# Attention and feed-forward sandwich: one inversion for the norm of the next input and of the output, input statistics in step 0

## The chip, the cores and the metric

The kernel runs on one core of a Trainium2 chip. The metric is the device time of one execution in microseconds (us). The core has five instruction queues that run side by side and meet in semaphores: TensorE (PE, matrix products and transposes; PEld is its weight load), VectorE (DVE), ScalarE (ACT), GpSimd (POOL) and SyncE (SP, which only issues DMA transfers).

## What is computed

Sixteen inputs of 256 tokens by 256 channels go through one attention layer and one feed-forward layer. Each layer is wrapped in two layer norms: one on what goes in, one on what comes out, before it is added to the residual.

```
x = x + _layernorm(attn(_layernorm(x)))
x = x + _layernorm(ffn(_layernorm(x)))

attn: q = x @ Wq.T (16 heads of 128); kv = x @ Wkv.T; kv_head = cumsum(x @ Wkvh.T * exp(cumsum of log_sigmoid(x @ Wg.T)))
      k, v = one key and one value row per token, scaled for each head by kv_head
      q, k = rope(q), rope(k); p = softmax(q k^T / sqrt(128), causal); out = (p v) @ Wout.T
_layernorm: (x - mean) / sqrt(var + 1e-5)
```

All 16 inputs are of one kind, so the attention part is a loop over 16 batches.

## The kernel before

Attention runs in 128 units, each a pair of heads: 16 batches of 8 pairs. The program is written out by hand as one stream of steps. A batch that begins at unit g0 (a multiple of 8) has steps s = 0 to 7, and every engine runs through the same steps in its own fixed order, with semaphores between. In step s a pair is projected and gets its cosine, the pair before is scored, the one before that goes through softmax, and older ones are transposed, multiplied with the values and projected out (table LAG).

Within one step the engines have this work for the pairs:

- TensorE: transposes of the probabilities (L944 to L946), value products, query projection, scores (L927, L929), output projection.
- VectorE: reciprocal of the sums (L1575), low half of the output (o_lo, L1597), query cosine (L1550), four splits of the probabilities (L1588), the maxima with the mask (L1562 to L1565).
- ScalarE: the exponents (L1229, L1231), the high halves, and the swap of the query halves (L1217, L1218).
- GpSimd: queries times sine (L597, waits for the swap), the rope addition (L607, which the scores wait for), normalise (L631, waits for L1575), keys times head scale (L620).

Around this stream lie the rarer pieces. Each has a step number in a table: FRONT for the batch that comes next, AHEAD for the batch after it (its norm is made early), TAIL for the outputs of the batch before. Of AHEAD there are the statistics of x (L1445, L1450 on VectorE; steps 3 and 4), the inversion (`invert_x`, L551 to L558 on GpSimd; step 5) and the normalisation on ScalarE (steps 6 and 7). Of TAIL there are the statistics of the attention output y (L1529, L1534; step 7), its inversion (`invert_y`, L575 to L582; step 1 of the next batch), its normalisation (steps 3 and 4) and the residual (L588; step 6). An inversion is four instructions on 2 columns, one for each block of 128 tokens: variance plus epsilon, mean times -1, the power -0.5, and the bias as the product. The mean and the inverse deviation of x and of y lie in the same tile `small`, not side by side.

A third stream makes the ternary weights of the feed-forward part, one chunk in two batches: on VectorE the steps above (L1622, even batches, step 1), below (L1630, even, start of step 2), decide (L1639, even, start of step 6), sign (L1646, odd, start of step 0), change (L1654) and finish (L1661, odd, steps 1 and 2), each on 1024 columns with two inputs in SBUF; on TensorE the transposes of the chunk in step 7 of odd batches (3 to 13). "Even" and "odd" are batch numbers, counted from 0; batch 8 begins at g0 = 64.

Of the kernel before, what the change touches and what calls it, by code (L numbers as in the profile page):

```python
# [25 lines left out]
ALU = mybir.AluOpType  # L26
AX = mybir.AxisListType

P = 128
# [25 lines left out]
             decay_a=3, decay_b=4, coef=5, weigh=5, sum=5, store=6, made=5, taken=5, turned=6, values_hi=7, values_lo=7, vh=7)  # L55
AHEAD = dict(stats_a=3, stats_b=4, invert=5, norm_a=6, norm_b=7)
FIRST = dict(stats_a=0, stats_b=0, invert=0, norm_a=1, norm_b=1, turn=2, split=2, split_lo=3, keys=3, gates=4,
# [26 lines left out]
def sandwich_kernel(nc, x, wq, wkv, wkvh, wg, wout, wgu, wproj, rope, out):  # L84
    ctx = ExitStack()
    with ctx:
# [20 lines left out]
        ones = sb("ones", [P, 1])  # L107
        minus_half = sb("minus_half", [P, NT])
        eps = sb("eps", [P, 1])
# [101 lines left out]
        ln1_stat = small[:, 48:60].rearrange("p (t a) -> p t a", a=6)  # L211
        ln1_agg = small[:, 60:64].rearrange("p (t a) -> p t a", a=2)
        ln1_rstd = small[:, 64:66]
        ln2_stat = small[:, 66:78].rearrange("p (t a) -> p t a", a=6)
        ln2_agg = small[:, 78:82].rearrange("p (t a) -> p t a", a=2)
        ln2_rstd = small[:, 82:84]
        gate_mark = small[:, 84:86]
        ln1_minus, ln2_minus = small[:, 90:92], small[:, 92:94]
        ln1_bias, ln2_bias = small[:, 86:88], small[:, 88:90]

# [91 lines left out]
        def front_at(g0, s, stage):  # L312

            if g0 == 0 and FIRST.get(stage) == s:
                return PAIRS
            if g0 + 2 * PAIRS < STEPS and AHEAD.get(stage) == s:
                return g0 + 2 * PAIRS
            if 0 < g0 and g0 + PAIRS < STEPS and FRONT.get(stage) == s:
                return g0 + PAIRS

        def tail_at(g0, s, stage):

            if g0 == STEPS and TAIL_LAST[stage] == s:
                return g0 - PAIRS
            back = TAIL[stage] // PAIRS
            if TAIL[stage] % PAIRS == s and g0 >= (back + 1) * PAIRS and (g0 < STEPS or back):
                return g0 - (back + 1) * PAIRS

        def head_count(g, j):
# [202 lines left out]
        def _(pool):  # L532
# [14 lines left out]
            def invert_x(c0):  # L547
# [10 lines left out]
                nc.gpsimd.tensor_tensor(ln1_bias, ln1_minus, ln1_rstd, ALU.mult).then_inc(ln1_biased, PAIRS)  # L558

            def key_sin(c0):  # L560

# [10 lines left out]
            def invert_y(c0):  # L572
# [4 lines left out]
                nc.gpsimd.tensor_tensor(ln2_minus, ln2_agg[:, :, 0], minus_one, ALU.mult).then_inc(ln2_neg, PAIRS)  # L577
                pool.wait_ge(ln2_eps, c0 + PAIRS)
                nc.gpsimd.tensor_tensor(ln2_rstd, ln2_rstd, minus_half[:, 0:NT], ALU.pow).then_inc(ln2_inv, PAIRS)  # L579
                pool.wait_ge(ln2_inv, c0 + PAIRS)  # L580
                pool.wait_ge(ln2_neg, c0 + PAIRS)
                nc.gpsimd.tensor_tensor(ln2_bias, ln2_minus, ln2_rstd, ALU.mult).then_inc(ln2_biased, PAIRS)  # L582
# [138 lines left out]
            def batch(g0, par, steps):  # L721
                for s in range(steps):
# [10 lines left out]
                    if not is_first(g0, s) and not is_first(g0, s - 2) and not is_first(g0, s - 3):  # L733
                        normalise(g0, s)
                        scale_keys(g0, par, s)
                    c0 = front_at(g0, s, "invert")
                    if c0 is not None:
                        invert_x(c0)
                    c0 = tail_at(g0, s, "invert")
                    if c0 is not None:  # L740
                        invert_y(c0)
# [404 lines left out]
        def _(act):  # L1146
# [16 lines left out]
            def norm_y(c0, tiles):  # L1163

                act.wait_ge(ln2_biased, c0 + PAIRS)
                act.wait_ge(x1_done, c0 + PAIRS)
# [748 lines left out]
```

## Time and profile before

| what | us |
|---|---|
| median of three runs (lowest, highest) | 1044.86 (1044.78, 1045.16) |
| the profiled execution, its own time | 1044.8 |
| its span, first to last instruction | 1043.0 |
| TensorE busy in the span | 1025.7 |
| GpSimd busy in the span | 937.8 |
| ScalarE and VectorE busy in the span | 868.6 and 824.8 |

TensorE's granted clock is 0.998 of full over the span. The attention batches run to about 823 us, the feed-forward part takes the rest. In a table of the profile "busy" is the time in which an instruction of the engine was under way; TensorE's products overlap each other, so that it can be busy throughout and still have waited a little before one of them. The timeline gives each instruction's start in us from the span's start.

### The profile page before, as it was taken

To read this page: it belongs to the slowest core of one execution; us is meant where nothing else is said; L and a number is where in the kernel's file an instruction comes from. 1 tells how busy PE (TensorE), PEld (TensorE's weight loads), DVE (VectorE), ACT (ScalarE), POOL (GpSimd) and SP (SyncE) were. 2 spreads that over 40 slices of the span, in tenths; PEclk is the share of its full clock that TensorE was granted. 3 is DMA by queue.
4 is the path that set the end of the run, shared out by engine and by line. 5 is a ranking of instruction groups with operands and counts; after the bars stand their busy time and mean duration, and the time that the engine had idled before them with its cause. 6 is when DMAs were issued, how large, how long until landed. Compare 5 with 4: busy or idle time off the path is not lost.

```text
span 1043.0 us, 25125 instructions
## 1 busy us (share of the span) xinstructions
PE 1025.7 (98%) x7859; PEld 985.8 (95%) x7859; DVE 824.8 (79%) x2824; ACT 868.6 (83%) x2399; POOL 937.8 (90%) x927
## 2 busy tenths in 40 slices
PE   7999999999999999999999999999999999999996
PEld 6899999999999999999999999999999899999996
DVE  6868798878887888888788888887777756766665
ACT  5978898989898889898988898888878777777774
POOL 4889999999999999999999999999999758888776
PEclk9999999999999999999999999999999999999999
DMA  7551111112111111221121112111131000000001
GB/s 262 186 183 42 41 63 41 43 52 72 42 32 62 62 42 33 65 66 44 38 76 43 42 52 62 50 34 63 31 113 31 2 1 12 30 24 22 21 22 41
DMA packets 35124, 58.56 MB, mean 56 GB/s; under 512 B 3136, under 2 KB 16000, under 8 KB 34688
## 3 DMA queue, kind: packets, MB, share of 16 engines
q1 hardware_dynamic: 34992, 56.96, 17.1%
q8 instruction: 63, 1.03, 0.4%
q14 instruction: 69, 0.57, 0.2%
HBM read 50.92 MB, written 9.18 MB: 58 GB/s over the span
## 4 chain that ended last, share of the span: by engine, by line
POOL 57%; PE 21%; issue 14%; DVE 1%; ACT 1%; POOLq 0%; ACTq 0%; DVEq 0%
POOL arena L597 15%; POOL arena L620 13%; POOL arena L631 13%; POOL arena L607 12%; PE psum L1015 12%; PE psum L1053 6%; PE psum L773 2%; POOL arena L579 1%; POOL arena L555 1%; POOL X L588 1%; PE psum L1028 1%; PE psum L1037 0%; POOL arena L563 0%; DVE pt_split L1588 0%; POOL wo_lo L648 0%
## 5 line engine op out<-in xcount | busy, mean ns | idle before, releaser
L631 POOL TENSOR_TENSOR arena<-arena 128x768 f32<-128x768 f32 x128 | 196.3, 1533 | 9.6 <-DVE arena L1575 9.0
L607 POOL TENSOR_TENSOR arena<-arena 128x512 f32<-128x512 f32 x128 | 174.6, 1364 | 10.0
L1588 DVE SCALAR_TENSOR_TENSOR pt_split<-psum,vh_col,pt_split 128x256 fp32r<-128x256 f32 (+1 forms) x512 | 177.0, 407 | 2.9 <-ACT pt_split L1248 2.7
L597 POOL TENSOR_TENSOR arena<-arena,tables 128x512 f32<-128x512 f32 x128 | 165.5, 1293 | 15.2 <-ACT arena L1218 14.4
L620 POOL TENSOR_TENSOR arena<-arena 128x512 f32<-128x512 f32 x127 | 163.0, 1284 | 0.0
L927 PE MATMUL psum<-arena 128*128 128x256 f32 x512 | 154.0, 382 | 3.8 <-POOL arena L607 2.5
L1229 ACT ACTIVATE arena<-arena 128x256 f32<-128x256 f32 x256 | 128.6, 502 | 28.4 <-DVE arena L1565 22.3
L773 PE MATMUL psum<-wo_hi,o_hi 128*128 128x256 f32 x512 | 152.0, 297 | 0.0
L773 PE MATMUL psum<-xt_lo,wq_hi 128*128 128x256 f32 x512 | 144.5, 282 | 0.0
L773 PE MATMUL psum<-xt_hi,wq_lo 128*128 128x256 f32 x512 | 144.4, 282 | 0.0
L773 PE MATMUL psum<-wo_hi,o_lo 128*128 128x256 f32 x512 | 144.2, 282 | 0.0
L773 PE MATMUL psum<-xt_hi,wq_hi 128*128 128x256 f32 x512 | 144.0, 281 | 0.0
L773 PE MATMUL psum<-wo_lo,o_hi 128*128 128x256 f32 x512 | 143.6, 281 | 0.0
L773 PE MATMUL psum<-pt_split,vals_hi 128*128 128x512 f32 (+1 forms) x512 | 142.3, 359 | 0.2
L1015 PE MATMUL psum<-xt_hi,wq_hi 128*128 128x256 f32 x512 | 125.6, 282 | 0.0
L1015 PE MATMUL psum<-xt_lo,wq_hi 128*128 128x256 f32 x512 | 124.4, 284 | 0.0
L1247 ACT ACTIVATE pt_split<-psum,vh_col 128x256 fp32r<-128x256 f32 x256 | 120.7, 472 | 0.1
L1217 ACT ACTIVATE arena<-psum 64x512 f32<-64x512 f32 x128 | 76.1, 595 | 46.6 <-DVE arena L1550 45.3
L1597 DVE TENSOR_TENSOR o_lo<-psum,o_hi 128x512 fp32r<-128x512 f32 x128 | 87.4, 682 | 33.9 <-ACT o_hi L1257 32.8
L929 PEld LDWEIGHTS psum<-arena 128*128 128x128 f32 x512 | 97.2, 190 | 13.3
L1563 DVE CUSTOM_DVE_ANT_0 arena<-psum,mask 128x256 f32<-128x256 f32 x256 | 107.0, 418 | 0.0
L1231 ACT ACTIVATE arena<-arena 128x128 f32<-128x128 f32 x256 | 99.4, 388 | 0.0
(193 smaller groups left out, 3415.8 us busy)
## 6 DMA issues: line engine op xcount, KB each, us to landing
arena<-kh_rows SPq DMA_DIRECT2D x127, 256.0 KB, 3.3
out<-spare SPq DMA_DIRECT2D x15, 256.0 KB, 2.2
arena<-w_rows SPq DMA_DIRECT2D x6, 512.0 KB, 4.7
X<-L_attn_Wout SPq DMA_DIRECT2D x1, 2048.0 KB, 14.5
X<-L_attn_x SPq DMA_DIRECT2D x1, 2048.0 KB, 12.3
arena<-L_attn_Wq SPq DMA_DIRECT2D x1, 1536.0 KB, 10.3
X<-L_attn_x SPq DMA_DIRECT2D x1, 1536.0 KB, 9.5
w_rows<-L_ffn_w_gate_up SPq DMA_DIRECT2D x3, 512.0 KB, 7.7
```

What stands on the lines that cost most here:

```text
L597: nc.gpsimd.tensor_tensor(swap, swap, spread, ALU.mult).then_inc(q_sined, 1)
L607: nc.gpsimd.tensor_tensor(q_rot[p % 2], q_cos[p % 2], q_swap[p % 2], ALU.add).then_inc(q_roped, 1)
L620: nc.gpsimd.tensor_tensor(k_head[p % 2], keys[par].unsqueeze(1).to_broadcast([P, HP, N]), kh_all[p % 4], ALU.mult).then_inc(k_scaled, 1)
L631: nc.gpsimd.tensor_tensor(tb, tb, r.unsqueeze(3).to_broadcast([P, HP, 3, P]), ALU.mult).then_inc(p_ready, 1)
L773: last = nc.tensor.matmul(o, a, b, start=start and i == 0, stop=stop and i == len(passes) - 1, skip_group_check=skip)
L927: nc.tensor.matmul(sj[:, 0:2 * P], q[:, j, P:N], kt[:, j, :], start=True, stop=True, skip_group_check=True)
L1015: last = nc.tensor.matmul(bank[c % 2 * 2 + half][:, j * N:(j + 1) * N], wgu_t[:, k, col:col + P], part[:, k, :], start=n == 0 and j == 0, ...
L1229: nc.scalar.activation(tb[:, j, 0:2 * P], tb[:, j, 0:2 * P], ACT.Exp, scale=-1.0, bias=nmax[p % 4][:, 2 * j:2 * j + 1], accum_out=rsum[p % ...
L1231: nc.scalar.activation(tb[:, j, 2 * P:3 * P], tb[:, j, 2 * P:3 * P], ACT.Exp, scale=-1.0, bias=nmax[p % 4][:, 2 * j + 1:2 * j + 2], accum_ ...
L1247: nc.scalar.activation(pt_hi[p % 2][:, j * N:(j + 1) * N], b[:, 0:N], ACT.Copy, scale=vh[:, 0, h:h + 1])
L1563: nc.vector.tensor_tensor_reduce(tb[:, j, 0:2 * P], S_BANK[j][:, 0:2 * P], mask[:, :], -1.0, -MASKED, ALU.add, ALU.min, nmax[p % 4][:, 2 * ...
L1588: last = nc.vector.scalar_tensor_tensor(pt_lo[p % 2][:, o], b[:, i], vh[:, t, h:h + 1], pt_hi[p % 2][:, o].bitcast(F32), ALU.mult, ALU.sub ...
```

## The change

The statistics of the next input go from steps 3 and 4 to step 0, and its inversion from step 5 to step 1, where that of the output already is. Batch 0 keeps the old steps (AHEAD_FIRST). Where both inversions fall in one step, which is in batches 2 to 13, they are made by one group of four instructions on 4 columns (`invert_both`); the means, variances and results of x and y lie side by side for that. In batch 1 there is only x to invert, in batches 14 and 15 and after them only y; these keep groups of two columns. ScalarE's normalisation of y then waits on the semaphore of the common group. `Y_ALONE` makes up the counts.

```diff
-AHEAD = dict(stats_a=3, stats_b=4, invert=5, norm_a=6, norm_b=7)
+AHEAD = dict(stats_a=0, stats_b=0, invert=1, norm_a=6, norm_b=7)
+AHEAD_FIRST = dict(stats_a=3, stats_b=4, invert=5, norm_a=6, norm_b=7)
+Y_ALONE = STEPS - 4 * PAIRS
...
+        ln_agg = small[:, 72:80].rearrange("p (t a) -> p t a", a=2)
+        ln_rstd, ln_bias, ln_minus = small[:, 80:84], small[:, 86:90], small[:, 90:94]
+        ln1_agg, ln2_agg = ln_agg[:, 0:NT, :], ln_agg[:, NT:2 * NT, :]
...
-            if g0 + 2 * PAIRS < STEPS and AHEAD.get(stage) == s:
+            if g0 + 2 * PAIRS < STEPS and (AHEAD if g0 else AHEAD_FIRST).get(stage) == s:
...
+            def invert_both(c0, y0):
+
+                pool.wait_ge(ln1_aggr, c0 + PAIRS)
+                pool.wait_ge(ln2_aggr, y0 + PAIRS)
+                at_least(pool, ln1_done, c0)
+                at_least(pool, ln2_done, y0 + PAIRS)
+                nc.gpsimd.tensor_tensor(ln_rstd, ln_agg[:, :, 1], eps[:, 0:1].to_broadcast([P, 2 * NT]), ALU.add)\
+                    .then_inc(ln1_eps, PAIRS)
+                nc.gpsimd.tensor_tensor(ln_minus, ln_agg[:, :, 0], minus_one[:, 0:1].to_broadcast([P, 2 * NT]), ALU.mult)\
+                    .then_inc(ln1_neg, PAIRS)
+                pool.wait_ge(ln1_eps, c0 + PAIRS)
+                nc.gpsimd.tensor_tensor(ln_rstd, ln_rstd, minus_half[:, :], ALU.pow).then_inc(ln1_inv, PAIRS)
+                pool.wait_ge(ln1_inv, c0 + PAIRS)
+                pool.wait_ge(ln1_neg, c0 + PAIRS)
+                nc.gpsimd.tensor_tensor(ln_bias, ln_minus, ln_rstd, ALU.mult).then_inc(ln1_biased, PAIRS)
...
+                    both = both_at(g0, s)
                     c0 = front_at(g0, s, "invert")
-                    if c0 is not None:
+                    if both:
+                        invert_both(*both)
+                    elif c0 is not None:
                         invert_x(c0)
                     c0 = tail_at(g0, s, "invert")
-                    if c0 is not None:
+                    if c0 is not None and not both:
                         invert_y(c0)
...
-                act.wait_ge(ln2_biased, c0 + PAIRS)
+                if c0 < Y_ALONE:
+                    act.wait_ge(ln1_biased, c0 + 5 * PAIRS)
+                else:
+                    act.wait_ge(ln2_biased, c0 - Y_ALONE + PAIRS)
```

The line numbers of the changed kernel are higher: GpSimd's by 24, VectorE's by 30. On VectorE, step 0 of batch 2 (with L1575 reciprocal, L1597 o_lo, L1550 cosine, L1588 splits) reads so before:

```order
L1575 RECIPROCAL arena<-arena 128x8 [waits p_exp]
L1597 TENSOR_TENSOR o_lo<-psum,o_hi 128x512 [waits o_hi_done]
L1550 TENSOR_TENSOR arena<-psum,tables 128x512 [waits q_roped,q_ready]
L1588 SCALAR_TENSOR_TENSOR pt_split<-psum,vh_col,pt_split 128x256 [waits o_ready,pt_hi_done]
L1588 SCALAR_TENSOR_TENSOR pt_split<-psum,vh_col,pt_split 128x128
L1588 SCALAR_TENSOR_TENSOR pt_split<-psum,vh_col,pt_split 128x256 [waits o_ready,pt_hi_done]
```

and so now:

```order
L1605 RECIPROCAL arena<-arena 128x8 [waits p_exp]
L1475 BN_STATS arena<-X 128x6 x2
L1480 BN_AGGR arena<-arena 128x2 [waits ln1_stats]
L1480 BN_AGGR arena<-arena 128x2
L1627 TENSOR_TENSOR o_lo<-psum,o_hi 128x512 [waits o_hi_done]
L1580 TENSOR_TENSOR arena<-psum,tables 128x512 [waits q_roped,q_ready]
L1618 SCALAR_TENSOR_TENSOR pt_split<-psum,vh_col,pt_split 128x256 [waits o_ready,pt_hi_done]
L1618 SCALAR_TENSOR_TENSOR pt_split<-psum,vh_col,pt_split 128x128
```

Two statistics and two aggregations have come between the reciprocal and o_lo (L1605 is the reciprocal now, L1627 o_lo, L1580 the cosine). On GpSimd, the end of step 1 and the beginning of step 2 of a batch read so before (L631 normalise, L620 keys, L575 to L582 the inversion of y, L597 and L607 the next step's queries):

```order
L631 TENSOR_TENSOR arena<-arena 128x768 [waits p_inv]
L620 TENSOR_TENSOR arena<-arena 128x512 [waits s_ready,kh_in1]
L575 TENSOR_TENSOR arena<-arena,eps 128x2 [waits ln2_aggr]
L577 TENSOR_TENSOR arena<-arena 128x2
L579 TENSOR_TENSOR arena<-arena,minus_half 128x2 [waits ln2_eps]
L582 TENSOR_TENSOR arena<-arena 128x2 [waits ln2_neg,ln2_inv]
L597 TENSOR_TENSOR arena<-arena,tables 128x512 [waits q_swapped]
L607 TENSOR_TENSOR arena<-arena 128x512 [waits s_ready,q_cosined,q_sined]
```

and so now:

```order
L655 TENSOR_TENSOR arena<-arena 128x768 [waits p_inv]
L644 TENSOR_TENSOR arena<-arena 128x512 [waits s_ready,kh_in1]
L574 TENSOR_TENSOR arena<-arena,eps 128x4 [waits ln1_done,ln2_aggr,ln2_done,ln1_aggr]
L576 TENSOR_TENSOR arena<-arena 128x4
L579 TENSOR_TENSOR arena<-arena,minus_half 128x4 [waits ln1_eps]
L582 TENSOR_TENSOR arena<-arena 128x4 [waits ln1_neg,ln1_inv]
L621 TENSOR_TENSOR arena<-arena,tables 128x512 [waits q_swapped]
L631 TENSOR_TENSOR arena<-arena 128x512 [waits s_ready,q_cosined,q_sined]
```

The four instructions have 4 columns and the first of them waits on four semaphores instead of one. On GpSimd the end of step 5 and the beginning of step 6 read so before, with the inversion of x (L551 to L558):

```order
L631 TENSOR_TENSOR arena<-arena 128x768 [waits p_inv]
L620 TENSOR_TENSOR arena<-arena 128x512 [waits s_ready,kh_in1]
L551 TENSOR_TENSOR arena<-arena,eps 128x2 [waits ln1_done,ln1_aggr]
L553 TENSOR_TENSOR arena<-arena 128x2
L555 TENSOR_TENSOR arena<-arena,minus_half 128x2 [waits ln1_eps]
L558 TENSOR_TENSOR arena<-arena 128x2 [waits ln1_neg,ln1_inv]
L597 TENSOR_TENSOR arena<-arena,tables 128x512 [waits q_swapped]
L607 TENSOR_TENSOR arena<-arena 128x512 [waits s_ready,q_cosined,q_sined]
```

and so now, without it:

```order
L655 TENSOR_TENSOR arena<-arena 128x768 [waits p_inv]
L644 TENSOR_TENSOR arena<-arena 128x512 [waits s_ready,kh_in1]
L621 TENSOR_TENSOR arena<-arena,tables 128x512 [waits q_swapped]
L631 TENSOR_TENSOR arena<-arena 128x512 [waits s_ready,q_cosined,q_sined]
L655 TENSOR_TENSOR arena<-arena 128x768 [waits p_inv]
```

The keys' product is followed by the next step's queries at once.

## Rows read from the trace of the kernel before

**Rows 1.** The page: busy us, share of the span and instructions of each engine.

```profile
PE 1025.7 (98%) x7859; PEld 985.8 (95%) x7859; DVE 824.8 (79%) x2824; ACT 868.6 (83%) x2399; POOL 937.8 (90%) x927
```

**Rows 2.** The windows of batches 1, 8 and 9, cut at their first score products.

```profile
core 0: us, PE busy (x) PEld busy (x) DVE busy (x) ACT busy (x) POOL busy (x), PEclk, DMA share, GB/s
72.43:122.66 50.23, 50.23 (x381) 48.17 (x379) 40.81 (x157) 43.50 (x131) 45.45 (x42) 1.00 0.14 43
426.57:477.13 50.56, 50.56 (x381) 48.28 (x379) 44.01 (x159) 44.02 (x132) 49.67 (x44) 1.00 0.19 54
477.13:527.88 50.75, 50.75 (x388) 48.66 (x387) 42.39 (x158) 45.43 (x134) 48.44 (x47) 1.00 0.16 49
```

**Rows 3.** TensorE's timeline, score products: start us, us, line, operation, tiles.

```profile
383.14 0.38 PE L927 MATMUL psum<-arena 128*128 128x256 f32 x1
...
426.57 0.38 PE L927 MATMUL psum<-arena 128*128 128x256 f32 x1
...
433.87 0.41 PE L927 MATMUL psum<-arena 128*128 128x256 f32 x1
...
470.67 0.48 PE L927 MATMUL psum<-arena 128*128 128x256 f32 x1
```

**Rows 4.** GpSimd's timeline, batches 7 and 8.

```profile
380.36 1.62 POOL L607 TENSOR_TENSOR arena<-arena 128x512 f32<-128x512 f32 x1
...
461.79 1.29 POOL L597 TENSOR_TENSOR arena<-arena,tables 128x512 f32<-128x512 f32 x1
...
467.09 1.29 POOL L597 TENSOR_TENSOR arena<-arena,tables 128x512 f32<-128x512 f32 x1
...
468.46 2.16 POOL L607 TENSOR_TENSOR arena<-arena 128x512 f32<-128x512 f32 x1
```

**Rows 5.** VectorE's timeline, steps 0 to 2 and the end of batch 8.

```profile
419.32 0.20 DVE L1575 RECIPROCAL arena<-arena 128x8 f32<-128x8 f32 x1 [2.13 <-ACT arena L1231]
...
420.46 0.69 DVE L1550 TENSOR_TENSOR arena<-psum,tables 128x512 f32<-128x512 f32 x1
...
425.01 0.20 DVE L1575 RECIPROCAL arena<-arena 128x8 f32<-128x8 f32 x1 [0.82 <-ACT arena L1231]
...
425.13 1.19 DVE L1622 TENSOR_TENSOR arena<-arena 128x1024 bf16<-128x1024 bf16 x1
...
426.23 0.68 DVE L1597 TENSOR_TENSOR o_lo<-psum,o_hi 128x512 fp32r<-128x512 f32 x1
...
426.83 0.68 DVE L1550 TENSOR_TENSOR arena<-psum,tables 128x512 f32<-128x512 f32 x1
...
429.86 1.22 DVE L1630 TENSOR_TENSOR arena<-arena 128x1024 bf16<-128x1024 bf16 x1
...
467.88 1.59 DVE L1646 TENSOR_TENSOR arena<-arena 128x1024 bf16<-128x1024 bf16 x1
```

**Rows 6.** GpSimd's timeline, step 5 of batch 8: the inverts of x, then L597.

```profile
453.63 0.20 POOL L551 TENSOR_TENSOR arena<-arena,eps 128x2 f32<-128x2 f32 x1
...
454.95 1.28 POOL L597 TENSOR_TENSOR arena<-arena,tables 128x512 f32<-128x512 f32 x1
```

**Rows 7.** ScalarE's timeline, second half of the swap in step 7 of batch 8.

```profile
466.17 0.59 ACT L1218 ACTIVATE arena<-psum 64x512 f32<-64x512 f32 x1
```

**Rows 8.** GpSimd's timeline, steps 1 and 2 of batch 8.

```profile
425.29 2.35 POOL L631 TENSOR_TENSOR arena<-arena 128x768 f32<-128x768 f32 x1
...
428.85 0.19 POOL L575 TENSOR_TENSOR arena<-arena,eps 128x2 f32<-128x2 f32 x1
...
429.18 0.71 POOL L579 TENSOR_TENSOR arena<-arena,minus_half 128x2 f32<-128x2 f32 x1
...
430.03 1.10 POOL L582 TENSOR_TENSOR arena<-arena 128x2 f32<-128x2 f32 x1
...
432.46 1.29 POOL L607 TENSOR_TENSOR arena<-arena 128x512 f32<-128x512 f32 x1
```

**Rows 9.** VectorE's timeline, statistics of y in step 7 of batch 8.

```profile
461.37 0.75 DVE L1529 BATCH_NORM_STATS2 arena<-arena 128x6 f32<-128x256 f32 x2
...
462.22 0.25 DVE L1534 BATCH_NORM_AGGREGATE arena<-arena 128x2 f32<-128x6 f32 x2
```

More of the change, by code:

```diff
@@ L107, in sandwich_kernel @@
         ones = sb("ones", [P, 1])
-        minus_half = sb("minus_half", [P, NT])
+        minus_half = sb("minus_half", [P, 2 * NT])
         eps = sb("eps", [P, 1])
@@ L211, in sandwich_kernel @@
         ln1_stat = small[:, 48:60].rearrange("p (t a) -> p t a", a=6)
[L212 to L216, printed above, removed]
+        ln2_stat = small[:, 60:72].rearrange("p (t a) -> p t a", a=6)
+        ln_agg = small[:, 72:80].rearrange("p (t a) -> p t a", a=2)
+        ln_rstd, ln_bias, ln_minus = small[:, 80:84], small[:, 86:90], small[:, 90:94]
+        ln1_agg, ln2_agg = ln_agg[:, 0:NT, :], ln_agg[:, NT:2 * NT, :]
+        ln1_rstd, ln2_rstd = ln_rstd[:, 0:NT], ln_rstd[:, NT:2 * NT]
+        ln1_bias, ln2_bias = ln_bias[:, 0:NT], ln_bias[:, NT:2 * NT]
+        ln1_minus, ln2_minus = ln_minus[:, 0:NT], ln_minus[:, NT:2 * NT]
         gate_mark = small[:, 84:86]
-        ln1_minus, ln2_minus = small[:, 90:92], small[:, 92:94]
-        ln1_bias, ln2_bias = small[:, 86:88], small[:, 88:90]
         x2_stat = small3[:, 0:12].rearrange("p (t a) -> p t a", a=6)
@@ L327, in tail_at, with both_at @@
                 return g0 - (back + 1) * PAIRS
+        def both_at(g0, s):
+            c0, y0 = front_at(g0, s, "invert"), tail_at(g0, s, "invert")
+            if c0 is not None and y0 is not None:
+                return c0, y0
         def head_count(g, j):
@@ L577, in invert_y @@
                 nc.gpsimd.tensor_tensor(ln2_minus, ln2_agg[:, :, 0], minus_one, ALU.mult).then_inc(ln2_neg, PAIRS)
-                pool.wait_ge(ln2_eps, c0 + PAIRS)
+                pool.wait_ge(ln2_eps, c0 - Y_ALONE + PAIRS)
                 nc.gpsimd.tensor_tensor(ln2_rstd, ln2_rstd, minus_half[:, 0:NT], ALU.pow).then_inc(ln2_inv, PAIRS)
-                pool.wait_ge(ln2_inv, c0 + PAIRS)
-                pool.wait_ge(ln2_neg, c0 + PAIRS)
+                pool.wait_ge(ln2_inv, c0 - Y_ALONE + PAIRS)
+                pool.wait_ge(ln2_neg, c0 - Y_ALONE + PAIRS)
                 nc.gpsimd.tensor_tensor(ln2_bias, ln2_minus, ln2_rstd, ALU.mult).then_inc(ln2_biased, PAIRS)
```

## The prediction

> **What bounds the kernel now.** I read the page first: TensorE is busy 98% of the span and GpSimd 90% [rows 1]. A share does not say which of them sets the time, so the second view is the table of windows, one window per batch, cut at the first score product of the batch. It shows 50.23 us for batch 1, 50.56 for batch 8 and 50.75 for batch 9, with GpSimd busy 45.45, 49.67 and 48.44 of them [rows 2]. TensorE is busy in all of each, so a batch can only be shorter by what TensorE loses between back-to-back products. Batch 1 is the reference without such a loss. Batch 9, like all odd batches from 3 to 13, has eight more products (388 against 381 records in the table, and their weight turning); 50.75 is 50.23 with those products. Batch 8 has the 381 of batch 1 and is 0.33 longer. So the even batches 2, 4, ..., 12 lose about 0.33 us each, 2 us in all, and this is the whole stock from which work taken off GpSimd can gain anything in the main loop.
>
> Where it is lost, the timelines show: the first product of the last score group of batch 8 starts at 470.67 [rows 3], 0.05 behind the end of GpSimd's addition L607, which starts at 468.46 and takes 2.16 [rows 4], where L597 of the same shape takes 1.29. So TensorE waited for it. The reason is VectorE's sign step L1646, at 467.88 to 469.47 [rows 5]: it has two inputs in SBUF. VectorE's step lasts until GpSimd's multiplication L597 (467.09 to 468.38) is over and then about 1.09 more, and GpSimd's addition starts to move only when it ends. I use this lock below: of two such instructions, the one that comes second waits for the first.
>
> **The change, part by part.** Steps are counted s = 0 to 7 in a batch.
>
> (a) Removed from GpSimd: the four instructions of the next input's norm in step 5 of twelve batches (2 to 13). In batch 8 they stand from 453.63 to 454.95 [rows 6], 1.32 us. What is gained is not 12 x 1.32, since GpSimd doesn't set the time there. L597 behind them then waits for ScalarE's swap, GpSimd's addition L607 meets VectorE's decide step, and by step 0 of the next batch at most the gap between swap and L597 is left: the swap ends at 466.76, L597 starts at 467.09 [rows 4, 7], 0.33, of which 0.08 is the usual semaphore delay. So L597, then the sign step, then the addition, each come 0.24 earlier, and of the loss of about 0.3 in each even batch 0.24 goes. Six times: -1.4 us.
>
> (b) Added to GpSimd: the four instructions of the output's norm in step 1 work on 4 columns instead of 2. An ordinary one of 2 columns takes 0.19, one of 512 columns 1.29 [rows 8], so two more columns cost nothing there. The power is another matter: 0.71 for 2 columns against 0.19 [rows 8]; no row shows it with 4. The bounds are 0 (the 0.52 above the ordinary one is all start-up) and +0.52 (it is all per column). The power's own row lies nearer to the ordinary one of 2 columns than to that of 512, where start-up is nearly all; I take +0.20, a little under the middle.
>
> (c) Moved on VectorE: both statistics and both aggregations of x go from steps 3 and 4 to step 0, right behind the reciprocal. The same four instructions for y run from 461.37 to 462.47, 1.10 us [rows 9]. In step 0 of batch 8 the reciprocal starts at 419.32 and the query's cosine at 420.46, with o_lo between [rows 5]. What follows a reciprocal starts 0.12 behind its start (425.01, 425.13), neighbours overlap by some 0.08, and the cosine follows o_lo by 0.60 (426.23, 426.83). With the four between, o_lo starts at 419.32 + 0.12 + 1.10 - 0.08 = 420.46 and the cosine at 421.06. That is +0.60. From there VectorE and ScalarE run without a gap: cosine, four splits, maxima, ScalarE's exponents, and VectorE's next reciprocal at 425.01, which waits 0.82 for them [rows 5], moves to 425.61. What waits for that is GpSimd's normalise L631 (425.29, 0.08 behind the reciprocal's end), which in these batches has no slack. The lock gives 0.08 back: the above step L1622 started at 425.13, before GpSimd's addition had ended at 425.21, and from 425.73 it runs at once. So normalise, keys, the inverts and L597 come 0.52 later, the below step L1630 with them, and the power's +0.20 is added, since L1630 and the bias multiplication (1.10 here, an ordinary one being 0.19 [rows 8]) queue behind it. The addition L607 of step 2 ends at 433.75, and the score product of TensorE behind it starts at 433.87 [rows 3, 8]: 0.12, of which 0.06 is delay. TensorE so loses 0.52 - 0.06 + 0.20 = 0.66 in each even batch from 2 to 12, six times: +4.0 us.
>
> (d) In odd batches the same delay is taken up. The addition L607 of step 2 of batch 7 ends at 381.98 [rows 4] and the score product starts at 383.14 [rows 3], 1.16 of slack, against 0.20 to 0.52 for the power and the 0.33 by which this addition (1.62) is held up already. Cost 0. TensorE's transposes of step 1 wait for VectorE's splits of step 0, which come 0.60 later in even batches. They don't stand among its waits for long anywhere now; I count them as 0 and a loss there with rival 3.
>
> (e) VectorE's steps 3 and 4 get shorter by the same 1.1 together. TensorE loses nothing in these steps, so this is worth 0. The waits on ln1_done and ln2_done are for work that ended in steps 7 and 4 of the batch before; they are free. Batch 0, the last two and the feed-forward part keep their instructions; batch 1, which loses nothing now, has only the x steps moved. No DMA moves.
>
> Do the statistics themselves hold GpSimd up? Beside those of y, which run from 461.37 to 462.12 [rows 9], GpSimd's L597 of 461.79 keeps its 1.29 [rows 4]; beside L1646 an instruction doesn't. The Trainium skill (page "SBUF — State Buffer", section "Who interferes with whom") says that a VectorE instruction with at most one SBUF input doesn't contend with GpSimd, and one with two does, whoever issues first holding the pair. By that (c) has no further term. Were it otherwise, up to 0.75 of statistics would be added to GpSimd in step 0 of six even batches, and the sum would be up to 4.5 us higher.
>
> **Sum.** -1.4 + 4.0 = +2.6 us against the profiled execution, which took 1044.80 (span 1043.0 and 1.8 around it) and stands 0.06 under the median of 1044.86. Forecast: 1047.4 us.
>
> **Rivals.**
> 1. The power costs the same for 4 columns as for 2. Then the losses are 6 x 0.46 = 2.8, less 1.4: +1.4, 1046.2 us. For it: 2 to 512 columns cost an ordinary instruction only 1.10. Against it: the power's 0.52 above the ordinary one. The Trainium skill ("GPSIMD Engine Reference", section "3.1 Elementwise — side-by-side cycle accounting") gives about 2.6 cycles per element for a two-input operation on top of the dispatch; by that two more columns are nothing, and the time is this rival's. No row shows the rate for a power.
> 2. The delay of (c) doesn't arrive, since the chain from cosine to normalise has slack that I don't see, and only (a) is left: -1.4, or 1043.4 us. This is faster, but by 0.14%; even the whole stock of 2.0 us gives 1042.8, 0.19%. Against it: L631 starts 0.08 behind the end of the reciprocal for which it waits [rows 5, 8], with no slack.
> 3. Slower by more: the power costs the whole 0.52, and the locks fall badly in odd batches too, a VectorE step of 1.09 coming ahead of a GpSimd instruction on which step 2 rests. The even batches then give 6 x 0.98 - 1.4 = +4.5, the odd ones up to 0.52 + 1.09 - 1.16 = 0.45 each, six times: 1049.3 to 1052.0 us. It decides when the delay in step 1 of an odd batch passes 1.1 us.
>
> **How the numbers follow.** About 0.2% (2.1 us) is what a measurement of this kernel can tell from no change. Forecast 0.42, of which 0.30 beyond +2.1 and 0.12 within; rival 1 0.22, within; rival 2 0.15, of which 0.05 faster than 0.2%, by a gain in a place where I see no loss now; rival 3 0.21, slower. So faster 0.05, same 0.44, slower 0.51. The range goes from rival 2 to the nearer part of rival 3: 1043.3 to 1049.8.
>
> **What would show it.** In the profile after: the statistics of x behind the reciprocal of step 0, and o_lo 0.6 later; the normalise of step 1 in even batches starting 0.6 later against TensorE's scores; the four-column power's duration (0.71 to 1.23), which settles (b); step 2's first score product 7.8 to 8.0 after that of step 1 in even batches, where it is 7.30 now [rows 3]; the last score group of even batches no longer right behind the end of an addition; odd batches at 50.75 as before, even ones at about 51.0. The prediction is wrong if 7.30 stays (rival 2), if the losses at the end of even batches stay, or if odd batches grow (rival 3).

## The result

The changed kernel takes 1046.51 us (median of 20 runs, 1046.11 to 1048.25) against 1044.91 for the kernel before (20 runs, taken beside it). The ratio is 1.0014, 95% interval 1.0008 to 1.0020: slower by 0.14%, or 1.5 us (1.6 between the medians). The profiled execution's span is 1044.5 us, before 1043.0.

The page of the changed kernel, busy us and shares of each engine (before: [rows 1]):

```profile
PE 1025.9 (98%) x7859; PEld 985.7 (94%) x7859; DVE 813.1 (78%) x2824; ACT 869.7 (83%) x2399; POOL 925.8 (89%) x879
```

GpSimd has 48 instructions and 12.0 us of work less, and the time went up. The windows of batches 1, 8 and 9, cut at their first score products, answer to [rows 2]:

```profile
core 0: us, PE busy (x) PEld busy (x) DVE busy (x) ACT busy (x) POOL busy (x), PEclk, DMA share, GB/s
72.50:122.73 50.23, 50.23 (x380) 48.16 (x379) 40.55 (x157) 43.56 (x131) 45.10 (x42) 1.00 0.13 43
427.04:477.81 50.77, 50.48 (x380) 48.22 (x379) 43.19 (x160) 44.20 (x133) 48.82 (x40) 1.00 0.16 54
477.81:528.54 50.73, 50.73 (x389) 48.63 (x388) 41.01 (x157) 45.33 (x134) 47.30 (x43) 1.00 0.16 48
```

Batch 1 is where it was, 50.23, batch 9 at 50.73 instead of 50.75. Batch 8 went from 50.56 to 50.77. GpSimd is busy 0.85 less in it, and TensorE, busy throughout before, now has 0.29 of idle time. The even batches from 4 to 12 all look like this (50.77 to 50.79), batch 2 less so (50.58 instead of 50.54).

TensorE's timeline says where in the batch. These are the first products of the score groups of steps 1, 2, 3 and of the last one of batch 8, against [rows 3]:

```profile
427.04 0.38 PE L954 MATMUL psum<-arena 128*128 128x256 f32 x1
...
434.79 0.48 PE L954 MATMUL psum<-arena 128*128 128x256 f32 x1 [0.29 <-POOL arena L631]
...
440.78 0.38 PE L954 MATMUL psum<-arena 128*128 128x256 f32 x1
...
471.51 0.38 PE L954 MATMUL psum<-arena 128*128 128x256 f32 x1
```

The score of step 2 follows that of step 1 by 7.75 us instead of 7.30, and waits 0.29 for GpSimd's addition (L631 in this kernel); the next follows by 5.99 instead of 5.90. This is a loss of 0.55 that was not there. At the end of the batch the last two intervals are 5.89 and 6.30 instead of 6.03 and 6.46: the loss of 0.3 that was there is gone. So a batch loses 0.55 and gets 0.30 back, where 0.33 was all that there was to get; 5 x 0.21 and 0.04 for batch 2 are +1.1 us.

VectorE in step 0 and 1 of batch 8, against [rows 5]. L1605 is the reciprocal, L1475 and L1480 the statistics and aggregations of x, L1627 o_lo, L1580 the cosine, L1652 above, L1660 below:

```profile
419.79 0.20 DVE L1605 RECIPROCAL arena<-arena 128x8 f32<-128x8 f32 x1 [2.13 <-ACT arena L1261]
...
419.91 0.70 DVE L1475 BATCH_NORM_STATS2 arena<-X 128x6 f32<-128x256 f32 x2
...
420.72 0.25 DVE L1480 BATCH_NORM_AGGREGATE arena<-arena 128x2 f32<-128x6 f32 x2
...
420.88 0.66 DVE L1627 TENSOR_TENSOR o_lo<-psum,o_hi 128x512 fp32r<-128x512 f32 x1
...
421.46 0.68 DVE L1580 TENSOR_TENSOR arena<-psum,tables 128x512 f32<-128x512 f32 x1
...
426.00 0.20 DVE L1605 RECIPROCAL arena<-arena 128x8 f32<-128x8 f32 x1 [0.83 <-ACT arena L1261]
...
426.12 1.18 DVE L1652 TENSOR_TENSOR arena<-arena 128x1024 bf16<-128x1024 bf16 x1
...
430.84 1.22 DVE L1660 TENSOR_TENSOR arena<-arena 128x1024 bf16<-128x1024 bf16 x1
```

And GpSimd in steps 1 and 2, against [rows 8], with one addition of step 0 ahead and, last, the addition at the end of the batch, against [rows 4]. L655 is the normalise, L574 to L582 are the common inversion, L621 and L631 the queries of the next step:

```profile
419.15 1.29 POOL L631 TENSOR_TENSOR arena<-arena 128x512 f32<-128x512 f32 x1
...
426.28 2.35 POOL L655 TENSOR_TENSOR arena<-arena 128x768 f32<-128x768 f32 x1 [0.18 <-DVE arena L1605]
...
429.84 0.21 POOL L574 TENSOR_TENSOR arena<-arena,eps 128x4 f32<-128x4 f32 x1
...
430.19 1.03 POOL L579 TENSOR_TENSOR arena<-arena,minus_half 128x4 f32<-128x4 f32 x1
...
431.36 0.77 POOL L582 TENSOR_TENSOR arena<-arena 128x4 f32<-128x4 f32 x1
...
432.08 1.29 POOL L621 TENSOR_TENSOR arena<-arena,tables 128x512 f32<-128x512 f32 x1
...
433.45 1.29 POOL L631 TENSOR_TENSOR arena<-arena 128x512 f32<-128x512 f32 x1
...
469.19 2.16 POOL L631 TENSOR_TENSOR arena<-arena 128x512 f32<-128x512 f32 x1
```

The four new instructions stand where the diff puts them, and o_lo starts 1.09 behind the reciprocal's start instead of 0.48, the cosine 1.67 instead of 1.14: 0.53 later. The next reciprocal is 6.21 behind the first instead of 5.69, the normalise 0.52 later, and the addition starts 13.66 behind the reciprocal of step 0 instead of 13.14: again 0.52. The delay of VectorE goes through the whole chain unchanged. The power takes 1.03 instead of 0.71, and yet nothing behind it is later by more than 0.52. The last row is a surprise: the addition that the sign step held up before (2.16) is held up just as long now, and yet the loss at the end of the batch is gone. It only begins earlier: it ends 5.73 behind the score product before it (465.63), where it ended 5.97 behind it, and TensorE isn't there before 5.89.

### The profile page after: what moved, and what is told of

It reads as the page before. It is cut to its first block, busy times and chain, and to the rows that moved or that the text cites. A ratio compares the mean times of both kernels' runs of the same rounds, so it can differ in the third digit from the quotient of the medians.

```text
span 1044.5 us, 25053 instructions
## 1 busy us (share of the span) xinstructions
PE 1025.9 (98%) x7859; PEld 985.7 (94%) x7859; DVE 813.1 (78%) x2824; ACT 869.7 (83%) x2399; POOL 925.8 (89%) x879
## 3 DMA queue, kind: packets, MB, share of 16 engines
q8 instruction: 63, 1.03, 0.4%
HBM read 50.92 MB, written 9.18 MB: 58 GB/s over the span
## 4 chain that ended last, share of the span: by engine, by line
POOL 56%; PE 21%; issue 15%; DVE 1%; ACT 1%; POOLq 0%; ACTq 0%; DVEq 0%
POOL arena L621 15%; POOL arena L644 14%; POOL arena L631 12%; POOL arena L655 12%; PE psum L1042 12%; PE psum L1080 6%; PE psum L800 2%; POOL arena L579 1%; PE psum L1055 1%; PE psum L1064 1%; POOL arena L587 0%; POOLq L303 0%; DVE pt_split L1618 0%; POOL X L612 0%; POOL wo_lo L672 0%
## 5 line engine op out<-in xcount | busy, mean ns | idle before, releaser
L655 POOL TENSOR_TENSOR arena<-arena 128x768 f32<-128x768 f32 x128 | 195.7, 1529 | 15.0 <-DVE arena L1605 14.9
L621 POOL TENSOR_TENSOR arena<-arena,tables 128x512 f32<-128x512 f32 x128 | 165.1, 1290 | 24.5 <-ACT arena L1248 23.7
L631 POOL TENSOR_TENSOR arena<-arena 128x512 f32<-128x512 f32 x128 | 173.0, 1352 | 10.0
L1627 DVE TENSOR_TENSOR o_lo<-psum,o_hi 128x512 fp32r<-128x512 f32 x128 | 87.3, 682 | 36.8 <-ACT o_hi L1287 36.0
```

The source lines that it names most:

```text
L621: nc.gpsimd.tensor_tensor(swap, swap, spread, ALU.mult).then_inc(q_sined, 1)
L631: nc.gpsimd.tensor_tensor(q_rot[p % 2], q_cos[p % 2], q_swap[p % 2], ALU.add).then_inc(q_roped, 1)
L655: nc.gpsimd.tensor_tensor(tb, tb, r.unsqueeze(3).to_broadcast([P, HP, 3, P]), ALU.mult).then_inc(p_ready, 1)
```

## The experiments

The table has the median of each kernel, that of the kernel before as it ran beside it on the same chip, and the ratio of the two with its interval, which is formed from all runs and can differ from the quotient of the medians (by 0.0005 in e1 and e3). The last column is the main loop in one profile of each, from the first score product of batch 2 to that of batch 15 (657.62 us before, 658.61 in the changed kernel, +1.0). Two profiles of one kernel show how far such numbers carry: e2 and e8 differ by 0.4 in the main loop and by 1.3 in what lies around it, e5 and e10 by 0.5 in the loop.

| kernel | us | before, beside it | ratio (95%) | main loop against before |
|---|---|---|---|---|
| changed | 1046.51 | 1044.91 | 1.0014 (1.0008 to 1.0020) | +1.0 |
| e1_stats_only | 1047.87 | 1044.73 | 1.0025 (1.0016 to 1.0034) | +3.0 |
| e2_merge_only | 1044.41 | 1044.73 | 0.9994 (0.9984 to 1.0003) | -1.2 |
| e8_merge_again | 1045.06 | 1045.52 | 0.9992 (0.9983 to 1.0001) | -0.8 |
| e3_wide_power | 1046.30 | 1044.73 | 1.0010 (1.0001 to 1.0019) | +0.4 |
| e4_above_later | 1046.68 | 1044.73 | 1.0017 (1.0008 to 1.0026) | +1.4 |
| e5_sign_later | 1043.64 | 1045.52 | 0.9980 (0.9971 to 0.9989) | -1.4 |
| e10_sign_again | 1043.32 | 1045.22 | 0.9982 (0.9973 to 0.9991) | -1.9 |
| e6_half_delay | 1044.83 | 1045.52 | 0.9995 (0.9986 to 1.0004) | -0.9 |
| e7_below_later | 1048.77 | 1045.52 | 1.0028 (1.0018 to 1.0039) | +3.1 |
| e9_merge_sign | 1044.80 | 1045.22 | 0.9996 (0.9987 to 1.0005) | -1.2 |
| e11_stats_sign | 1046.79 | 1045.22 | 1.0014 (1.0005 to 1.0023) | +1.4 |

### Each half of the change by itself

```diff
-AHEAD = dict(stats_a=3, stats_b=4, invert=5, norm_a=6, norm_b=7)
+AHEAD = dict(stats_a=0, stats_b=0, invert=5, norm_a=6, norm_b=7)
```

> The kernel before with only the statistics of the next input moved to step 0 (its inversion stays in step 5, nothing is merged). Theory (late VectorE): the score product of step 2 in even batches 2 to 12 follows that of step 1 by about 7.7 to 7.8 us instead of 7.30, the losses of 0.3 at the end of even batches stay, and the time is 6 x 0.46 to 0.55 = 2.8 to 3.3 us above before, about 1048. Rival (the wider inversion is what costs): 7.30 stays and the time is that of before, 1044.9.

The time went up by 3.1 us between the medians (2.6 by the ratio). Batch 8's window and its score product of step 2, which starts 7.75 behind that of step 1 (427.84):

```profile
core 0: us, PE busy (x) PEld busy (x) DVE busy (x) ACT busy (x) POOL busy (x), PEclk, DMA share, GB/s
427.84:478.94 51.10, 50.78 (x381) 48.28 (x379) 44.31 (x160) 44.27 (x133) 50.21 (x44) 1.00 0.16 53
```

```profile
435.59 0.48 PE L928 MATMUL psum<-arena 128*128 128x256 f32 x1 [0.29 <-POOL arena L608]
```

The same wait of 0.29 as in the changed kernel, without any merging, and the next interval is again 6.00. The last intervals stay at 6.08 and 6.42, the old loss. The even batches 4 to 12 take 51.10 to 51.13 instead of 50.56 to 50.58, batch 2 takes 50.92 instead of 50.54. The statistics in step 0 cost 0.55 in each of these five and 0.38 in batch 2, and this is all of the new loss.

For the other half, the common inversion stays in step 1 and the statistics of x are made in steps 3 and 4 of the batch before (only the main part of the edit is shown; batches 0 and 1 have places of their own):

```diff
+            if stage in ("stats_a", "stats_b") and g0 >= PAIRS:
+                if g0 == PAIRS and s == 6:
+                    return 4 * PAIRS
+                if g0 > PAIRS and g0 + 3 * PAIRS < STEPS and AHEAD_FIRST[stage] == s:
+                    return g0 + 3 * PAIRS
```

> The changed kernel with the statistics of x left in steps 3 and 4, but one batch earlier, so that the common inversion in step 1 stays and VectorE's step 0 is free of them (batches 0 and 1 keep the old places). Theory (late VectorE): 7.30 to 7.36 between the scores of steps 1 and 2 in even batches, no loss at their end, all main-loop batches at their floor of 50.23 and 50.73: 1042.9 to 1043.2 us, about 1.9 below before. Rival (the power's 0.32 us more reach TensorE): about 7.56 in even batches, 6 x 0.26 us more, 1044.5 us.

Batch 8 went to 50.31, the intervals to 7.30 and 5.95 in step 2 and to 5.89 and 6.31 at the end:

```profile
core 0: us, PE busy (x) PEld busy (x) DVE busy (x) ACT busy (x) POOL busy (x), PEclk, DMA share, GB/s
425.75:476.06 50.31, 50.31 (x380) 48.20 (x379) 43.08 (x159) 44.04 (x132) 48.59 (x40) 1.00 0.18 54
```

Merging is a gain in the main loop of 1.2 us in the trace. Not all of the theory's 1.9 came: batch 9, and only that one, takes 50.99 instead of 50.76, the loss being in its last three intervals (51.03 in the second profile of the same kernel, and 50.99 in e9_merge_sign, which has the same edit); what makes it so is open. The time moved by less than the main loop, 0.3 us, and its interval includes 1.

> The same kernel as in the run with the merged inversion and x's statistics in steps 3 and 4 of the batch before, once more, to make its interval against before narrower. From its trace's main loop, 1.2 to 1.5 us shorter than that of before: 1043.5 to 1044.0, ratio 0.9987 to 0.9993.

Once more under before, by 0.5 us, and by 0.8 in the main loop, with batch 9 again the long one (51.03). Each interval includes 1; that merging alone is faster than before is likely from the two runs and the traces, but not shown by either time.

### The longer power

```diff
-                nc.gpsimd.tensor_tensor(ln2_rstd, ln2_rstd, minus_half[:, 0:NT], ALU.pow)
+                nc.gpsimd.tensor_tensor(ln2_wide, ln2_wide, minus_half[:, :], ALU.pow)
```

> The kernel before with one thing changed: the power in the inversion of y works on 4 columns, two of them filler, and takes about 1.02 instead of 0.70 us. Theory (the bias product behind it waits for VectorE's below step anyway): 7.30 stays, 1044.9 within 0.3. Rival (GpSimd's 0.32 reach TensorE in even batches, where the slack is 0.06): about 7.56, 6 x 0.26 = 1.6 us more, 1046.5.

GpSimd in step 1 of batch 8, the power (L581), the bias product (L584) and the queries behind it, and VectorE's below step:

```profile
429.92 1.03 POOL L581 TENSOR_TENSOR arena<-arena,minus_half 128x4 f32<-128x4 f32 x1
...
431.09 0.77 POOL L584 TENSOR_TENSOR arena<-arena 128x2 f32<-128x2 f32 x1
...
431.81 1.29 POOL L599 TENSOR_TENSOR arena<-arena,tables 128x512 f32<-128x512 f32 x1
```

```profile
430.58 1.22 DVE L1632 TENSOR_TENSOR arena<-arena 128x1024 bf16<-128x1024 bf16 x1
```

The power takes 1.03 us, so two more columns cost 0.32. The below step starts at 430.58, while the power is under way until 430.95, and takes its usual 1.22 us: it doesn't wait for the power. The bias product does wait for the below step, which ends at 431.80; it takes 0.77 instead of 1.10 and ends 0.06 behind it. So the 0.32 come out of a wait. The scores of step 2 follow at 7.30; the interval after that grew from 5.90 to 5.93 to 5.96. In the main loop it is +0.4 us, a quarter of the 1.6 of the rival. The time as measured is 1.6 us above before between the medians and 1.0 by the ratio, with an interval from 0.1 to 2.0, which neither excludes the theory's 0.3 nor the rival's 1.6; for the even batches the trace decides.

Batch 15, outside this loop, shows the other side. No ternary step runs there, so nothing makes the bias product wait but the power itself:

```profile
783.34 1.02 POOL L581 TENSOR_TENSOR arena<-arena,minus_half 128x4 f32<-128x4 f32 x1
...
784.49 0.20 POOL L584 TENSOR_TENSOR arena<-arena 128x2 f32<-128x2 f32 x1
```

The product takes its 0.20, GpSimd's addition ends 0.05 ahead of the score product that it releases, and the first interval of batch 15 is 6.18 instead of 5.88. Here 0.30 of the power's 0.32 reach TensorE. So the longer power is free where the below step covers it, or where GpSimd has slack (the odd batches and batch 14 didn't grow), and costs its time where there is neither. The main loop and batch 15 are +0.7 together. The first score product of batch 2 is 0.5 later too, but so is the first one of all (20.48, before 20.02), ahead of any inversion of y, and e2 and e8, one kernel, differ by as much there: that isn't the power.

### How much delay, how much loss

One of the two statistics instructions goes out of step 0 of the changed kernel into step 6 of the batch before:

```diff
+            if stage == "stats_a" and g0 + 3 * PAIRS < STEPS and s == 6:
+                return g0 + 3 * PAIRS
+            if stage == "stats_a" and g0:
+                return None
```

> The changed kernel with one of the two statistics instructions of x (0.35 us) taken out of step 0 and put into step 6 of the batch before; the other and both aggregations stay in step 0. Theory (VectorE's lateness in step 0 reaches TensorE one for one): the interval between the scores of steps 1 and 2 of even batches goes from 7.75 to about 7.40, the changed kernel's 1046.5 to about 1044.7 (6 x 0.35 less = 2.1, some of it kept by the step of 5.99 behind). Rival (any instruction ahead of o_lo costs the same, by a lost slot): 7.75 stays and 1046.5.

In batches 4 to 12 the score of step 2 follows at 7.42 to 7.43 and the batch takes 50.45 to 50.51:

```profile
core 0: us, PE busy (x) PEld busy (x) DVE busy (x) ACT busy (x) POOL busy (x), PEclk, DMA share, GB/s
426.21:476.67 50.46, 50.46 (x380) 48.21 (x379) 43.14 (x159) 44.14 (x132) 48.71 (x40) 1.00 0.18 54
```

Taking 0.35 us out of VectorE's step 0 gives 0.32 back, nearly one for one. The time is that of the kernel before (ratio 0.9995, interval with 1 in it). The rival falls.

### The locks

GpSimd's and VectorE's instructions with two inputs in SBUF hold each other up. Three edits move one such VectorE step each. The first two start from the changed kernel.

```diff
-WSTEP = dict(cast=5, sum=6, scale=7, above=9, below=10, decide=14, sign=16, change=17, finish=18, turn=23, copy=23,
+WSTEP = dict(cast=5, sum=6, scale=7, above=11, below=10, decide=14, sign=16, change=17, finish=18, turn=23, copy=23,
```

> The changed kernel with VectorE's above step (two inputs in SBUF, 1.19 us) in step 3 of even batches instead of step 1, where it holds up GpSimd's normalise (2.35 instead of 1.47 us). Theory (delay of the statistics plus this lock is what makes step 2 late): normalise takes 1.47, GpSimd gets 0.88 back, which is more than the 0.46 to 0.55 lost, so 7.75 goes back to 7.30 and the time to 1043.0 to 1043.5. Rival (the delay reaches TensorE by another way than the normalise): 7.75 stays and the time is that of the changed kernel, 1046.5.

GpSimd's normalise of step 1 and of step 3, and TensorE's score product two steps behind the second:

```profile
426.30 1.47 POOL L655 TENSOR_TENSOR arena<-arena 128x768 f32<-128x768 f32 x1 [0.18 <-DVE arena L1605]
...
432.90 1.29 POOL L631 TENSOR_TENSOR arena<-arena 128x512 f32<-128x512 f32 x1
...
439.50 2.40 POOL L655 TENSOR_TENSOR arena<-arena 128x768 f32<-128x768 f32 x1
```

```profile
446.53 0.48 PE L954 MATMUL psum<-arena 128*128 128x256 f32 x1 [0.24 <-POOL arena L631]
```

In step 1 it went as the theory has it: the normalise takes 1.47, the score of step 2 follows at 7.30. But the lock went along with its step. The normalise of step 3 now takes 2.40, and the intervals behind grow from 5.89, 5.89 and 6.59 to 6.28, 6.00 and 6.69. The loss moved by two steps and stayed as large (50.84 against 50.77), and the time with it: 1046.68 where 1043.0 to 1043.5 was expected. What I had left out is what the step does where it goes: the slack of step 3 is 0.73 in the kernel before (GpSimd's addition ends at 439.04, the score product starts at 439.77), and the step brings a delay of 0.9.

```diff
-WSTEP = dict(cast=5, sum=6, scale=7, above=9, below=10, decide=14, sign=16, change=17, finish=18, turn=23, copy=23,
+WSTEP = dict(cast=5, sum=6, scale=7, above=9, below=11, decide=14, sign=16, change=17, finish=18, turn=23, copy=23,
```

> The changed kernel with VectorE's below step (two inputs in SBUF, 1.22 us) at the start of step 3 of even batches instead of step 2, where it holds up GpSimd's bias product (0.77 instead of 0.20 us). Theory (that step hides the longer power and is the last link before step 2): the bias takes 0.20, GpSimd's queries of step 2 come 0.57 earlier and 7.75 goes to 7.30; the lock moves to step 3, where the slack is 0.73, and may take 0.3 to 0.4 back there, so 1043.5 to 1046. Rival (the lock on the normalise alone counts): 7.75 stays.

```profile
431.25 1.03 POOL L579 TENSOR_TENSOR arena<-arena,minus_half 128x4 f32<-128x4 f32 x1
...
432.41 0.20 POOL L582 TENSOR_TENSOR arena<-arena 128x4 f32<-128x4 f32 x1
...
432.57 1.29 POOL L621 TENSOR_TENSOR arena<-arena,tables 128x512 f32<-128x512 f32 x1
...
439.25 2.15 POOL L631 TENSOR_TENSOR arena<-arena 128x512 f32<-128x512 f32 x1
```

The bias product takes 0.20, the queries of step 2 start at once, and the score follows at 7.30: that much is as foreseen, and it shows that the wait for the below step was a link of the chain to step 2. It wasn't the only one: without the above step, and with the bias product still waiting (1.11), e4 came to 7.30 as well. But the addition of step 3 takes 2.15, and the three intervals behind are 6.07, 6.36 and 6.01 instead of 5.90, 5.89 and 5.88. This costs more than it brings: +3.1 us against before in the main loop, where the changed kernel has +1.0, and 1048.77 us where 1043.5 to 1046 was expected. My estimate of what comes back, 0.3 to 0.4 per batch, was half of the real 0.8.

```diff
-WSTEP = dict(cast=5, sum=6, scale=7, above=9, below=10, decide=14, sign=16, change=17, finish=18, turn=23, copy=23,
+WSTEP = dict(cast=5, sum=6, scale=7, above=9, below=10, decide=14, sign=17, change=17, finish=18, turn=23, copy=23,
```

This one is an edit of the kernel before.

> The kernel before with VectorE's sign step (two inputs in SBUF) at the start of step 1 of odd batches instead of step 0, where it stands in the way of GpSimd's addition (2.16 instead of 1.29 us). Theory (this lock makes the loss at the end of even batches): the last score of even batches follows the one before by 5.89 instead of 6.03 to 6.07 and the next by 6.31 instead of 6.40 to 6.46; odd batches have 1.16 us of slack in step 2 and take the sign step in; about 1.7 us less than before, 1043.1. Rival (the loss comes from GpSimd's work summing up over the batch): the intervals stay and the time is that of before.

> The kernel before with the sign step in step 1 of odd batches, once more, beside the others of this call: 1.5 to 1.9 us under before, even batches at 50.34 to 50.37 in the trace instead of 50.56.

It is the fastest of all: 1.9 us under it, twice, with intervals clear of 1. The window of batch 8 in the second run, and GpSimd's addition L607 at the end of that batch and one step later:

```profile
core 0: us, PE busy (x) PEld busy (x) DVE busy (x) ACT busy (x) POOL busy (x), PEclk, DMA share, GB/s
425.65:475.90 50.25, 50.25 (x380) 48.19 (x379) 43.16 (x159) 44.04 (x132) 49.10 (x44) 1.00 0.17 54
```

```profile
467.61 1.29 POOL L607 TENSOR_TENSOR arena<-arena 128x512 f32<-128x512 f32 x1
...
473.18 2.15 POOL L607 TENSOR_TENSOR arena<-arena 128x512 f32<-128x512 f32 x1
```

The addition of step 0 takes 1.29 where it took 2.16 [rows 4]. The lock hits the addition one step later, 2.15, where odd batches have slack, and they stay at 50.73. So the loss at the end of even batches can be cured with GpSimd's work unchanged: the rival, that this work alone makes it, falls. But the meeting alone doesn't make it either. In the changed kernel and with merging alone the same addition takes 2.15 to 2.17 in all six even batches, and the loss is gone there too (5.89 and 6.30 or 6.31), because GpSimd begins it about 0.24 earlier against the score product before. It took both, the 0.87 of the lock and GpSimd's lateness, and taking away either was enough.

### Do the gains add up?

First the merged inversion with the statistics of x one batch earlier, and the later sign step (both diffs above).

> Merged inversion with x's statistics one batch earlier in steps 3 and 4, and VectorE's sign step in step 1 of odd batches. Theory: either edit alone takes the loss at the end of even batches away, so together they give what the later sign step gives alone (about 1.9 us under before); what can still be won is the 0.1 us per even batch that is left with it, so 1.9 to 2.3 under before. Rival (the gains of merging and of the sign step add up): 3 us or more under before.

They don't, and the expected 1.9 to 2.3 us under before missed too: it is 0.4, and the main loop is 1.2 us under before, as with merging alone, even batches at 50.28 to 50.46, batch 9 again at 50.99. Beside it the later sign step by itself took 1043.32 us (e10). On top of it the merging, as made here, costs 1.5 us: 0.7 in the main loop, most of it in batches 2 and 9, the rest around it. Why those batches lose isn't known. With the later sign step there was nothing left for the merging to win.

> The kernel before with two edits: statistics of x in step 0, sign step in step 1 of odd batches; no merged inversion. Theory (in the changed kernel the merging does no more than take away the loss at the end of even batches, and the statistics cost 0.55 in step 2): the scores of step 2 follow at 7.75 and 5.99, the last ones at 5.89 and 6.31, as in the changed kernel, and the time is the changed kernel's, 1.2 to 1.6 us over before. Rival (the shorter GpSimd work is worth more than that): the time is clearly above the changed kernel's, 3 us over before as with the statistics alone.

It is the kernel before with two of the edits above, statistics in step 0 and the sign step in step 1, and no merged inversion. The window of its batch 8 and of the changed kernel's are the same, 50.76 and 50.77:

```profile
core 0: us, PE busy (x) PEld busy (x) DVE busy (x) ACT busy (x) POOL busy (x), PEclk, DMA share, GB/s
427.02:477.78 50.76, 50.48 (x380) 48.21 (x379) 43.42 (x159) 44.21 (x133) 49.31 (x44) 1.00 0.17 53
```

The odd batches, which now take the sign step in as well as the statistics' delay, are at 50.79 to 50.81 (batch 5 at 50.73) instead of 50.73, which makes the main loop 0.4 longer than the changed kernel's. The ratio to before is 1.0014 for both kernels. With the end of the even batches cleared by other means, the four instructions that the merging saves in each of twelve batches are worth nothing that shows.

## Why the prediction was right, and where its sizes were off

The forecast was 1047.4 us, slower, in a range of 1043.3 to 1049.8; measured were 1046.51, +1.5 us where +2.6 was the sum. Direction and main mechanism hold: the statistics make VectorE late in step 0, and this reaches TensorE in step 2 of even batches. Of its signs, the interval of 7.75 and the even batches of 50.77 stay a little under the 7.8 to 8.0 and the 51.0 that were given. By its chances, slower than the 2.1 us that can be told from no change had 0.51 and within them 0.44; +1.5 lies within. Its terms were 0.4 (a) and 1.2 (b) too slow and 0.3 (c) too fast, 1.3 us too slow together. By its steps:

- **Which engine sets the time.** TensorE does, and GpSimd only in the even batches. Confirmed by batch 1 and the odd batches, which stayed within 0.1 of 50.23 and 50.73 under every edit, batch 9 with the statistics one batch earlier excepted.
- **(a), forecast -1.4.** The losses at the end of even batches went altogether, 0.30 each, -1.8 us. I let only 0.24 go, since L597 still waits for the swap, and L597 and the addition did come just 0.24 earlier against the score product before them. But the interval to the last score group needed only 0.14 of that (6.03 to 5.89), and another 0.16 went in the interval behind (6.46 to 6.30), which the prediction didn't count by itself. The lock on the addition stayed at 2.16; the later sign step shows that removing it is the other cure.
- **(b), forecast +0.20 per batch for the power.** This is the step that failed, and not in the power's duration (+0.32, inside the bounds of 0 and 0.52) but in what lies beside it. I had VectorE's below step queue behind the power, so that the two add up. It starts while the power is under way, and the bias product waits for its end in any case; the power fills that wait. On the path of even batches it costs 0 to 0.06 in the run with the longer power; in batch 15 of that run, with neither a below step nor slack, it costs 0.30.
- **(c), forecast +0.52 for the delay, 0.46 at TensorE.** The delay is 0.52 in the trace, at the cosine (0.53), the reciprocal, the normalise and the addition. I had come to 0.52 by another way, 0.60 at the cosine less 0.08 that the lock was to give back; nothing is given back (the above step starts 0.12 behind the reciprocal and takes 1.18, as before), and the cosine is only 0.53 later, since o_lo starts 1.09 behind the reciprocal where I had 1.14 and the cosine 0.58 behind o_lo where I had 0.60. That two slips cancel is luck. TensorE loses 0.45 in the interval and another 0.10 in the one behind, 0.55; this second part I did not have. Half of the delay gives back 0.32. In batch 2, where VectorE had more idle time in step 0, the cosine comes only 0.33 later and the loss is 0.32; I had counted it like the others.
- **(d) and (e), forecast 0.** Right: the odd batches didn't grow. In batch 9 the slack before the score product of step 2 fell from 1.16 to 0.70.
- **The sum.** With the measured terms, -1.8 + 5 x 0.55 + 0.32 = +1.3. The main loop in the trace has +1.0 from batch 2 to 15, the span +1.5, the medians +1.6. The rest of about 0.5 lies at the edges of the loop, where hardly anything is changed. Two profiles of one kernel (e2 and e8) differ by more than that there, so one profile can't tell whether it comes from the change; it stays open.

The first rival gave 1046.2 and lies nearest to the result, but its reason was another: it let the power cost the same for 4 columns as for 2, and it costs 0.32 more. What it had right is that next to none of this arrives, and that is again luck: the below step happened to cover it.

The Trainium skill's rule on contention (page "SBUF — State Buffer", section "Who interferes with whom") lets a VectorE instruction with one SBUF input run beside GpSimd, and the changed kernel agrees: beside the statistics, which have one, GpSimd's addition of 419.15 keeps its 1.29 us. The same page of the Trainium skill (section "SBUF: two separate sides") says that whichever of a VectorE operation with two SBUF inputs and a GpSimd one starts first has the ports for the whole instruction. That doesn't fit the power: it started first (430.19, until 431.22), and the below step of 430.84 took its usual 1.22.

## What to carry to other kernels

Work that is taken off an engine is worth no more than the waits that the bounding engine still has for it; add up these waits first (here 2.0 us of 1044.9), and look what makes each of them. Here a meeting of two instructions and the amount of work made them together; moving one instruction cured them for nothing, while taking work off cured them at the price of what came with it. Instructions that make the merging possible have a place too: four short ones ahead of a chain that has no slack cost more than the merging saved. A VectorE step that is moved takes its lock along, so the slack of the place where it goes must be larger than the delay that it brings. An instruction gets longer for free when the one behind it waits for something else; without such a wait, and without slack, it cost its time (batch 15 of e3).

## What the runs showed of the hardware

- A GpSimd power on 128x2 takes 0.70 us and on 128x4 1.02, 0.16 a column, where an addition or product goes from 0.19 to 0.20.
- A VectorE operation with two SBUF inputs (128x1024, bf16) and a GpSimd operation on 128x512 or 128x768 hold each other up: where they met, the GpSimd one took up to 2.17 for 1.29 or up to 2.45 for 1.47, and the step took that along to every place to which it was moved (e4, e5, e7). A GpSimd power on 4 columns, 1.03 long, doesn't hold such a VectorE operation up: 1.22 beside it (changed kernel, e3), 1.22 too in the kernel before, where the power ends 0.03 behind its start.
